# Edge network of a GNN kernel: its own stage of ten loads merged into the later return stage, with the scatters that ran beside it put behind that stage's gathers

## The reference

```python
# layer 0: attention over 53125 edges, linear-attention mixer, then a mixture of 8 experts:
x = x + ffn0(...)        # route each node to one of 8 experts, 256 -> 1024 -> 256, come back, scale
# layer 1: per edge, a small network turns 10 length features into one radial weight   <-- "edge network"
r = silu(emb @ fc_w1 / sqrt(10)) @ fc_w2 * const           # emb: (53125, 10)
# ... messages x[src] * (angular * r) summed by dst, mixer, and a second mixture of experts whose gate
# is a graph attention over ANOTHER edge list (32768 edges plus self loops), which needs those edges
# sorted by dst                                             <-- "pairs"
```

## Time and profile before

| | us |
|---|---|
| median of three runs | 3129.1 |
| lowest, highest run | 3125.21, 3131.22 |
| profiled execution, its own time | 3132.5 |
| span of the profiled execution | 3130.8 |
| PE busy | 2334.8 (75%) |
| DVE busy | 2012.6 (64%) |
| POOL busy | 1760.6 (56%) |
| ACT busy | 1372.2 (44%) |

### The profile page before, as it was taken

One profiled execution on the slowest core, in us unless ns is written; L12 is line 12 of the kernel. 1 busy time (PEld: TensorE's weight loads), 2 busy tenths in 40 slices (PEclk: granted clock), 3 DMA queues, 4 the chain that ended last, 5 costly groups with the idle time before them and its releaser, 6 DMA issues. The chain is left out here.

```text
span 3130.8 us, 41052 instructions
## 1 busy us (share of the span) xinstructions
PE 2334.8 (75%) x11127; PEld 1532.2 (49%) x11128; DVE 2012.6 (64%) x4054; ACT 1372.2 (44%) x3793; POOL 1760.6 (56%) x1789
## 2 busy tenths in 40 slices
PE   3996777777776666599969577777777788888781
PEld 2554555555554555166614223233336677776660
DVE  4564999999998887011063489999994632222588
ACT  0222566556543443321126488888882222222230
POOL 1544778777772045667751477777762057777100
PEclk8998888888887555799969799998998789999895
DMA  3213666666660100133221233333321121111004
GB/s 102 54 39 113 205 202 202 208 205 201 203 191 1 56 30 16 47 117 104 71 75 51 61 98 100 103 100 100 100 83 17 32 55 36 36 36 36 16 1 175
DMA packets 163880, 287.79 MB, mean 92 GB/s; under 512 B 55384, under 2 KB 99421, under 8 KB 163662
## 3 DMA queue, kind: packets, MB, share of 16 engines
q0 software_dynamic: 79568, 187.15, 21.5%
q1 hardware_dynamic: 71834, 79.09, 8.1%
q10 hardware_dynamic: 12260, 18.94, 1.7%
HBM read 248.79 MB, written 36.25 MB: 91 GB/s over the span
## 5 line engine op out<-in xcount | busy, mean ns | idle before, releaser
L2333 PE MATMUL cv_ps<-cv_msg,cv_hot 128*128 128x512 f32 x880 | 435.5, 652 | 165.1 <-DVE acc L2383 125.0
L2320 POOL DMA_INDIRECT cv_x<-x_tab,e_src x440 | 447.4, 1017 | 195.8 <-issue 94.8
L960 POOL DMA_INDIRECT at_kv<-kv_tab,e_src x440 | 464.6, 1056 | 154.8 <-issue 85.9
L2754 POOL DMA_INDIRECT gs_h<-h_tab,fc_q x312 | 294.4, 944 | 177.9 <-issue 93.6
L2333 PEld LDWEIGHTS cv_ps<-cv_msg,cv_hot 128*128 128x128 f32 x880 | 179.6, 210 | 420.7 <-ACT cv_msg L2346 216.3
L2004 POOL DMA_INDIRECT pairs<-gating_pair,gating_place x288 | 275.8, 958 | 159.3 <-issue 69.1
L2346 ACT ACTIVATE cv_msg<-cv_x,factors 128x64 f32<-128x64 f32 x1320 | 356.5, 333 | 0.0
L2383 DVE TENSOR_TENSOR acc<-acc,cv_ps 128x256 f32 x880 | 307.5, 413 | 38.1 <-PE cv_ps L2333 31.4
L2344 ACT ACTIVATE cv_msg<-cv_x,factors 128x256 f32<-128x256 f32 x440 | 217.8, 495 | 127.4 <-DMA cv_x<-x_tab,e_src 127.4
L1096 PE MATMUL at_a<-at_kv,at_hot_e 128*128 128x264 f32 x880 | 253.7, 418 | 7.3 <-DVE at_kv L1169 5.0
L1071 PE MATMUL at_q<-q_parts,at_hot_n 128*128 x1320 | 214.4, 314 | 40.2 <-DVE at_kv L1153 32.3
(11 more groups left out here) (545 smaller groups left out, 4610.8 us busy)
## 6 DMA issues: line engine op xcount, KB each, us to landing
x_w<-in_L_ffn_w SPq DMA_DIRECT2D x16, 1024.0 KB, 8.1
at_rel_row<-e_rel_rows SPq DMA_DIRECT2D x55, 256.0 KB, 4.7
experts_out<-gs_y ACTq DMA_DIRECT2D x20, 512.0 KB, 2.7
x_y<-experts_out SPq DMA_DIRECT2D x20, 512.0 KB, 4.8
at_kv<-kv_tab,e_src POOLq DMA_INDIRECT x440, 3.8
cv_x<-x_tab,e_src POOLq DMA_INDIRECT x440, 2.8
kv_tab<-p_qkv SPq DMA_DIRECT2D x25, 256.0 KB, 2.0
gs_h<-h_tab,fc_q POOLq DMA_INDIRECT x312, 2.3
```

The lines of the kernel that those rows point to most:

```text
L960: nc.gpsimd.indirect_dma_start(out=kv[:, t % (RING * Q4), 0:2 * D], out_offset=None, in_=kv_tab, in_offset=bass.IndirectOffsetOnAxis(ap=e. ...
L2320: nc.gpsimd.indirect_dma_start(out=xg[:, i % RT, u, :], out_offset=None, in_=x_tab, in_offset=bass.IndirectOffsetOnAxis(ap=e.src[:, t:t + ...
L2333: nc.tensor.matmul(ps[u % R][:, :], hot[:, i % 2, u, :], msg[:, i % 2, u, :], start=True, stop=True).then_inc(summed, 1)
L2754: nc.gpsimd.indirect_dma_start(out=hg[:, i % RT, u, :], out_offset=None, in_=h_tab, in_offset=bass.IndirectOffsetOnAxis(ap=e.src[:, i * U ...
```

## The change

The stage `radial0` is gone. Its ten loads are done in the return stage ahead of the other sixteen, so the return stage now does loads 0 to 25 (SP issues 2 to 25; 0 and 1 are still loaded in the sort stage). The 48 scatters of turns 6 to 11 move into the expert stage, which now does turns 6 to 29 instead of 12 to 35, again 192 scatters. The last six turns, 48 scatters, are issued by POOL in the return stage, after its 25 gathers and before the four `ef_angular` gathers.

```diff
-def radial0(nc, k, ef, pairs, pair, place_i):
-
-    with Scope(nc) as s:
-        ps_h, ps_r = ef.banks(s, "ro_ef")
-        scatter = Scatter(s, "ro_sc_", SORT_SCATTER, RADIAL_SCATTER)
-        with nc.Block() as block:
-            @block.sync
-            def _(sp):
-                ef.load(sp, 2, ef.FIRST)
-
-            @block.scalar
-            def _(act):
-                ef.activate(act, ps_h, ps_r, 0, ef.FIRST)
-
-            @block.tensor
-            def _(pe):
-                ef.multiply(pe, ps_h, ps_r, 0, ef.FIRST)
-
-            @block.gpsimd
-            def _(pool):
-                total = ef.R * ef.FIRST
-                scatter.run(nc, k, pool, pairs, pair, place_i,
-                            pace=lambda n: [(ef.hid, n * total // (scatter.turns * U))] if n * total >= scatter.turns * U else [])
...
-        scatter = Scatter(s, "x0_sc_", RADIAL_SCATTER, C2 // U)
+        scatter = Scatter(s, "x0_sc_", SORT_SCATTER, RETURN_SCATTER)
...
-def return0(nc, k, out_buf, slot_i, factor, ef, angular, stats):
+def return0(nc, k, out_buf, slot_i, factor, ef, angular, stats, pairs, pair, place_i):
...
+        scatter = Scatter(s, "re_sc_", RETURN_SCATTER, C2 // U)
         with nc.Block() as block:
             @block.sync
             def _(sp):
-                ef.load(sp, ef.FIRST, ef.LOADS)
+                ef.load(sp, 2, ef.LOADS)
                 for j in range(2):
                     sp.wait_ge(ef.stored[j], 16 * ((ef.LOADS + 1 - j) // 2))
 
             @block.tensor
             def _(pe):
-                ef.multiply(pe, ps_h, ps_r, ef.FIRST, ef.LOADS)
+                ef.multiply(pe, ps_h, ps_r, 0, ef.LOADS)
 
             @block.scalar
             def _(act):
-                ef.activate(act, ps_h, ps_r, ef.FIRST, ef.LOADS)
+                ef.activate(act, ps_h, ps_r, 0, ef.LOADS)
...
+                scatter.run(nc, k, pool, pairs, pair, place_i)
                 ef.angles(pool, angular)
...
-RADIAL_SCATTER = SORT_SCATTER + 6
+RETURN_SCATTER = C2 // U - 6
...
-    FIRST = 10
```

More of the change, by code:

```diff
@@ L3204, in program @@
                     sort_and_route(nc, k, a["L1_ffn_edge_index"], pairs2, pair, place_i, slots, slot_i, factor, ef)
-                    radial0(nc, k, ef, pairs2, pair, place_i)
                     experts0(nc, k, a, slots, slots_out, pairs2, pair, place_i)
                     stats = LayerStats(nc, t, k, "n2_")
-                    return0(nc, k, slots_out, slot_i, factor, ef, angular, stats)
+                    return0(nc, k, slots_out, slot_i, factor, ef, angular, stats, pairs2, pair, place_i)
                     stats.finish()
```

## The result

The changed kernel is faster by half a percent, which is clear of chance: 3113.22 us median of 10 runs (3102.95 to 3120.5) against 3129.76 us of the kernel before (3121.48 to 3133.98), ratio 0.9949 with a 95% interval of 0.9936 to 0.9963. That is 16.5 us less; 3104 was forecast, in a range of 3094 to 3116. The profiled execution took 3113.56 us, span 3111.8 us, beside 3132.5 and 3130.8 before.

What follows compares the result with a forecast made beforehand. POOL was taken to bound the radial stage, PE and ACT's chain the return. Removing 66.5 us and adding 41.0 gives -25.5 us, from the median 3129.1 to 3103.6, forecast as 3104, range 3094 to 3116.

Steps and rivals of the forecast that it cites:

- its own case: Return stage: POOL arrives last, at 1707 to 1713, giving 3100 to 3107 us; chance 0.58.
- rival 1: Return stage: clock stays low longer, 5 to 8 cold loads beyond the first; 3105 to 3115 us, chance 0.18.
- POOL's terms: Return stage: 48 scatters, landing wait, four angular gathers and drain, putting POOL's end at 1710.4.
- The prediction's bounds for the barrier: Return's end: 1707.5 if DVE slows no scatters, 1713 if it slows all; 1710.4 taken between.
- PE's terms: Return stage: ten more loads on PE, whose barrier would come at 1704.5 with three cold loads beyond the first.
- 102.1 + 3.49 n: PE's time in us for 26 return loads; n counts loads at the low clock beyond the first.
- Rival 3: Return stage: clock never rises, so PE ends late and the kernel is slower, 3174 us; chance 0.03.
- rival 4: Return stage: POOL's scatters are not slowed and drain quickly; 3098 us, or 3093 with at most one extra cold load; chance 0.13.
- The lock: Return stage: port pair shared by VectorE and GpSimd is exclusive, the loser fully blocks; would speak against the change.
- rival 2: Return stage: POOL stands still while DVE works, stage +67.1 us, no net change, 3130 us; chance 0.03.
- the return's barrier moves from 1669.4: Return's end: moves to the later of PE's 1704.5 and POOL's 1710.4, so the stage grows by 41.0 us.

Runs made afterwards that it cites:

- `loads_only`: Against the kernel before: only the ten loads moved to the return, the radial stage keeping its 48 scatters; 3169.24 us, ratio 1.0112.
- `return64`: Against the changed kernel: 64 scatters in the return and 176 in the experts; 3114.45 us, ratio 0.9948 to the kernel before.
- `ahead_fill`: Changed kernel with 64 scatters in sort, 32 in return, the experts' first 12 unpaced, 8 constant matmuls ending PE's experts part; 3079.85 us, ratio 0.9847.

## Why the prediction was right, and where its size was off

**The mechanism was right.** One stage of 66.5 us went, the return grew to POOL's end, and POOL, not PE, was last, in all three profiled executions. The return was put at 121.1 us and measured 123.1 to 123.6. The size was off: 25.5 us were forecast and 16.5 measured. The median, 3113.22 us, lies within the range but 9 us over the forecast and over the 3100 to 3107 that the prediction gave to its own case. That part of the range was there for rival 1, which did not come, so it is in part luck that the number is inside.

**POOL's terms.** The 48 scatters were put at 1.62 us beside DVE and 1.263 alone, and 21 of them beside DVE; measured 1.59, 1.26 and 21. Small terms were off, all in the tail. From the end of the last scatter to the first angular gather it was put at 1.3 us and was 1629.88 - 1626.47 = 3.4, since the last scatter landed late: the longest from issue to landing took 4.3 us in the return (1625.52 + 4.3 = 1629.8), where the median in the radial stage was 2.1. The angular gathers went at 1.27 us each, so 4.8 us in place of 5.4, and from their end to the drain it was 3.0 in place of 2.7. The drain was put at 4.7 us and took 6.3. The prediction took a value between four rows and left out that the sort's 6.0 us belonged to 73 indirect DMAs (48 scatters, 25 others), so that 77 had to take more; it is one law (below). These four make +2.1 - 0.6 + 0.3 + 1.6 = +3.4 us; the last scatter ended 105.5 us into the stage where 107.0 was forecast (1626.47 - 1521.0; 1696.3 - 1589.3), and the stage was 2 us longer. The scatters' error hid part of the tail's. The prediction's bounds for the barrier, 1707.5 and 1713, are 1707.7 and 1713.3 by its own terms.

**PE's terms.** 102.1 + 3.49 n held: 101.7 with n = 0 here, and in `loads_only` the stage was 111.7 with n = 2. Rival 1, a late clock, did not come (n = 0 three times). By the sum POOL's end would hide n up to 5; the trace of `return64` shows n = 1 hidden. Rival 3 was not seen. For rival 4 nothing speaks: the scatters were slowed like the gathers.

**The lock.** 21 scatters went through while DVE worked, the longest 1.6 us instead of 0.96. The Trainium skill, SBUF — State Buffer, in "two separate sides", tells of a port pair that GpSimd and VectorE lock from one another for a whole instruction; it says so of a VectorE instruction in a 2-port mode, or of one with two SBUF inputs beside a GpSimd instruction that reads SBUF, which the prediction left out. The trace agrees with a wait for the one DVE instruction that is running, and not with POOL standing still for DVE's whole stretch; rival 2 falls. It can be read scatter by scatter:

```profile
1578.83 1.73 DVE L474 BATCH_NORM_STATS2 n_parts<-X 128x6 f32<-128x256 f32 x5
1579.94 0.96 POOL L1981 DMA_INDIRECT pairs<-gating_pair,gating_place  x1 [0.30 <-issue]
1580.48 1.47 DVE L1555 TENSOR_TENSOR re_y<-re_y,factor 128x1280 f32<-128x1280 f32 x1
1581.20 1.59 POOL L1981 DMA_INDIRECT pairs<-gating_pair,gating_place  x1 [0.30 <-issue]
```

The scatter that began under TENSOR_TENSOR ended 0.84 us behind it (1582.79 and 1581.95). All 20 that began under a TENSOR_TENSOR, a COPY_PREDICATED or a TENSOR_SCALAR ended 0.77 to 0.87 us behind it. The three that began under BATCH_NORM_STATS2 took 0.95 to 0.96 us, as alone. What a scatter pays is thus at most what is left of the DVE instruction under which it begins, and it depends on the instruction's kind. TENSOR_SCALAR has one SBUF input and delayed scatters too; whether it ran in a 2-port mode no run shows.

**The step that was mis-sized** is, beside the tail, "the return's barrier moves from 1669.4". That 80.1 us return was one draw. Over four executions it is 78.3 us, since before the change the edge network's chain decided the return in three of them (DVE in the fourth) and the cold loads counted, while after the change POOL's end covers them. The prediction carried n for the changed stage and forgot that the stage before had it too.

**The account.** Means over four profiled executions before and three after: radial -66.6, experts 271.8 to 270.8, return 78.3 to 123.3, behind the return 1460.7 to 1463.5. The sum is -66.6 - 1.0 + 45.0 + 2.8 = -19.8 us; these executions' own times differ by 3130.4 - 3111.1 = 19.3, and the other 0.5 us lie ahead of the radial stage. The interval of the ratio reaches from 20.0 to 11.6 us. So against these executions the forecast of 25.5 was off by some 2 us at POOL's end, 1.8 of the return before, and some 3 us behind the return, less 1.0 in the experts. The other 3 us down to the 16.5 of the medians are not accounted for; they lie within the interval.

**What stays open** is the 3 us behind the return. They lie for the most part in the convolution (`convolve`), which the change does not touch. Its window before, then after:

```profile
1750.70:2351.10 600.40, 435.51 (x880) 179.61 (x880) 536.82 (x1101) 496.59 (x1760) 447.44 (x440) 0.90 0.33 97
```

```profile
1731.30:2336.10 604.80, 438.08 (x880) 180.55 (x880) 536.94 (x1101) 496.57 (x1760) 449.19 (x440) 0.90 0.33 96
```

In the six profiles of kernels that have the radial stage it took 598.6 to 601.3 us (mean 600.3), in the eight without it 601.3 to 604.8 (mean 603.2). That is more than chance would easily give, but no experiment varied a cause, and the traces name none. ACT waited there for its gathers 125.7 to 131.1 us (mean 128.5) in the six and 128.4 to 135.9 (mean 131.5) in the eight. The small stage ahead of it (`mixer_matrix1`) took 20.1 to 25.9 us in both kinds of kernel, by how long the granted clock stood at 0.50 in it. The first profile of the changed kernel had 25.9 against 20.2 before; with the convolution's 4.4 more, and less in other stages, that is why its total showed only 19 of 25 us.

## What to carry to other kernels

In a program of stages with barriers, ask of each stage which engine arrives last and by how much. Moving work between stages pays only if the engine that receives it has slack there or the stage that gives it up disappears altogether: here each half of the move lost 24 us or more and both together won 16. Then ask again who is last, since the next gain lies there: taking POOL's tail off two stages gave another 26 to 32 us by the ratios (0.9866, 0.9855 and 0.9847 against 0.9949). And before resting a sum on the length of one stage, look at that stage in more than one execution.

## What the runs showed of the hardware

- POOL's drain at a block's end grows with the number of indirect DMAs that POOL issued in the block: 29, 48, 61, 73, 77, 89 and 93 of them took 2.41, 3.97, 5.02, 6.02, 6.33, 7.32 and 7.63 us, 82 to 83 ns each. It lengthens the stage only where POOL arrives last. The law does not hold for the experts: 6.6 us for 192 and 5.3 for 176, though 16 DMAs are again 81 ns each. The cause is open. Pauses alone are not it: in the sort POOL waited 48.9 us for DVE between scatters, and its 73 DMAs keep to the law.
- The same 128 matmul records of the return took PE 64.3 to 78.8 us of busy time from one execution to the next, as the clock rose to its 2.4 GHz level after one, three, four or five loads of small matmuls, though PE was busy without a gap.
- The granted clock fell while PE was busy without a gap: in `ahead_fill` between 1510 and 1512, behind a warm start at 1509.07, under the edge network's multiplies by `w1`.
- An indirect DMA that POOL began under one of DVE's TENSOR_TENSOR, COPY_PREDICATED or TENSOR_SCALAR instructions ended 0.77 to 0.87 us behind that instruction (20 of 20 scatters in the changed kernel's first profile), and took 0.95 to 0.96 us under BATCH_NORM_STATS2 (3 of 3), as without DVE.
